# Attribute sums of a graph kernel, regrouped from two-strip pieces into three-strip units behind single tiles

## What is computed

```
h   = relu(layernorm(x));  H = batchnorm(h @ W.T + b)
deg = 1 + segment_sum(1, dst);  dinv = rsqrt(deg)
x   = x + relu(segment_sum(H[src] * dinv[src] * dinv[dst], dst) + H * dinv * dinv)
h   = relu(layernorm(x))
agg = segment_sum(edge_attr, dst)          # 206250 x 128 attributes, fp32
x   = x + (relu(relu([h, agg, u] @ W1 + b1) @ W2 + b2) @ W3 + b3)
```

## Time and profile before

| what | us |
|---|---|
| median of 3 runs | 1004.99 (1004.8 to 1006.06) |
| the profiled execution, its own time | 1005.95 |
| its span in the profile | 1004.2 |
| PE busy | 916.0 (91%), 9255 matmul instructions |
| POOL, DVE, ACT busy | 619.2, 578.5, 502.0 |
| strip sums of attributes, L1178, busy | 167.7 in 2240 instructions (attr_hot), 74.0 in 1000 (rows_hot) |
| strip sums of gathered rows, L1192, busy | 36.9 in 1000 instructions |

### The profile page before, as it was taken

The page is one execution under the profiler, slowest core; times in us unless marked ns, Lnnn a source line. Parts: engine busy times, 40 slices in busy tenths (PEclk is TensorE's granted clock), DMA queues, the critical chain, the costliest instruction groups (busy, mean ns, idle before and its releaser), DMA issues. The chain is left out here.

```text
span 1004.2 us, 23679 instructions
## 1 busy us (share of the span) xinstructions
PE 916.0 (91%) x9255; PEld 659.4 (66%) x9255; DVE 578.5 (58%) x1319; ACT 502.0 (50%) x867; POOL 619.2 (62%) x610
## 2 busy tenths in 40 slices
PE   2479559999999999999999999999999999997687
PEld 1357436777777777777777777777777777776455
DVE  6673756556555555556555655555565555542944
ACT  2135546455455555555555555555555555541485
POOL 5574562577777777777776177777777777710014
PEclk9567769999999999999999999999999999998989
DMA  7000464465565566565566355665655655623203
GB/s 183 14 1 1 130 211 157 135 205 169 187 204 173 182 203 194 164 201 178 178 201 189 127 171 186 204 194 165 201 177 178 202 182 174 204 64 92 53 21 108
DMA packets 87065, 154.65 MB, mean 154 GB/s; under 512 B 10967, under 2 KB 36885, under 8 KB 87005
## 3 DMA queue, kind: packets, MB, share of 16 engines
q1 hardware_dynamic: 71004, 121.11, 37.5%
q0 software_dynamic: 16000, 32.80, 10.9%
HBM read 147.46 MB, written 6.41 MB: 153 GB/s over the span
## 5 line engine op out<-in xcount | busy, mean ns | idle before, releaser
L957 POOL DMA_INDIRECT gathered<-scaled_h_table,index x500 | 534.6, 1069 | 232.4 <-issue 144.1
L969 ACT CAST counts_sb<-ps_counts 128x588 f16<-128x588 f32 x560 | 384.6, 688 | 367.7 <-PE ps_counts L1148 351.4
L1154 PE MATMUL ps_product<-counts_sb,table_sb 128*128 128x240 f16 x2744 | 436.0, 264 | 0.0
L1148 PE MATMUL ps_counts<-key_hot,lo_hot 128*128 128x294 bf16 x1120 | 329.2, 298 | 14.4 <-DVE key_hot L1031 12.3
L1154 PEld LDWEIGHTS ps_product<-counts_sb,table_sb 128*128 128x128 f16 x2744 | 266.0, 97 | 43.8 <-ACT counts_sb L969 0.2
L1031 DVE TENSOR_TENSOR key_hot<-key,iota_key 128x1176 bf16<-128x1176 f16 x280 | 213.4, 762 | 0.0
L1178 PE MATMUL ps_sums<-attr,attr_hot 128*32 128x128 f32 x2240 | 167.7, 280 | 2.9 <-DMA attr<-in_edge_attr_dram 2.9
L1089 DVE TENSOR_TENSOR acc<-acc,ps_product 128x96 f32 (+1 forms) x137 | 37.4, 273 | 223.2 <-PE ps_product L1208 187.2
L1148 PEld LDWEIGHTS ps_counts<-key_hot,lo_hot 128*128 128x128 bf16 x1120 | 111.4, 101 | 72.1 <-issue 24.1
L1026 DVE TENSOR_TENSOR lo_hot<-src_lo,iota_key 128x512 bf16<-128x512 f16 x280 | 118.6, 424 | 50.5 <-PE ps_counts L1148 50.4
L1178 PEld LDWEIGHTS ps_sums<-attr,attr_hot 128*32 128x32 f32 x2240 | 106.8, 110 | 48.6 <-issue 48.2
(11 more groups left out here) (219 smaller groups left out, 715.9 us busy)
## 6 DMA issues: line engine op xcount, KB each, us to landing
attr<-in_edge_attr_dram SPq DMA_DIRECT2D x80, 1280.0 KB
gathered<-scaled_h_table,index POOLq DMA_INDIRECT x500
acc<-in_x_dram SPq DMA_DIRECT2D x4, 768.0 KB, 9.0
scaled_h_table<-table_sb SPq DMA_DIRECT2D x12, 256.0 KB, 2.3
xs<-in_x_dram SPq DMA_DIRECT2D x12, 256.0 KB, 5.3
out_dram<-y_ring SPq DMA_DIRECT2D x12, 256.0 KB, 2.3
attr<-in_edge_attr_dram SPq DMA_DIRECT2D x2, 320.0 KB, 3.3
attr<-in_edge_attr_dram SPq DMA_DIRECT2D x1, 640.0 KB
```

The lines of the kernel that those rows point to most:

```text
L957: pool.indirect_dma_start(gathered[:, n % GATHERS, g, :], None, table, bass.IndirectOffsetOnAxis(ap=index[:, s * CG + g, t:t + 1], axis=0) ...
L969: act.copy(counts_sb[s % 2][:, :, 2 * k * WT:(2 * k + 2) * WT] .rearrange("p h (t n) -> p t h n", n=WT), ps_counts[n % 2][:, :, 0:KEYS].re ...
L1148: pe.matmul(ps_counts[pair % 2][:, c, 0:KEYS], lo_hot[:, b, part, :, c], key_hot[:, b, part, :, c], start=True, stop=True).then_inc(built, 1)
L1154: ins = pe.matmul(ps_product[side][:, 0:SLOTS], table_sb[:, h, low, :], counts_sb[side][:, h, :], start=(part == 0), stop=(part == 2 * NB ...
```

## The change

SUMS is now keyed by the tile q instead of the pair p, and its entries are (what, t, g), single matmuls. The 20 matmuls of a chunk are taken in the order of t and then g, three at a time (TRIPLES, seven of them, the last with two), and one such triple stands behind each of the tiles q = 2 to 8 (j = 0), 14 to 20 (j = 1) and 26 to 32 (j = 2). `sum_rows` stands behind q = 10, 12, 24, 35 and 37, where it stood behind q = 11, 13, 25, 35 and 37. Placements and `turn_product` keep their places. `sum_attr` takes one (t, g) and loses its loop. The number of matmuls is the same.

```diff
-        ALL, FIRST, SECOND = range(0, CG), range(0, CG // 2), range(CG // 2, CG)
-        SUMS = {1: [(0, FIRST, 0), (0, FIRST, 1)], 2: [(0, FIRST, 2), (0, FIRST, 3), (0, FIRST, 4)],
-                3: [(0, SECOND, 0), (0, SECOND, 1)], 4: [(0, SECOND, 2), (0, SECOND, 3), (0, SECOND, 4)],
-                5: [(3, ALL, 0)], 6: [(3, ALL, 1)],
-                7: [(1, FIRST, 0), (1, FIRST, 1)], 8: [(1, FIRST, 2), (1, FIRST, 3), (1, FIRST, 4)],
...
+        TRIPLES = [range(n, min(n + 3, CT)) for n in range(0, CT, 3)]
+        SUMS = {first + k: [(j, n // CG, n % CG) for n in triple]
+                for j, first in enumerate((2, 14, 26)) for k, triple in enumerate(TRIPLES)}
+        SUMS |= {q: [(3, t, 0)] for t, q in enumerate((10, 12, 24, 35, 37))}
...
-                            def sum_attr(s, k, a, held, loads, j, groups, t, first):
-                                if groups[0] == 0 and t == 0:
+                            def sum_attr(s, k, a, held, loads, j, t, g, first):
+                                if t == 0 and g == 0:
...
-                                for g in groups:
-                                    ins = pe.matmul(ps_sums[g * W:(g + 1) * W, 1, 0:P], hot[:, t, g, :],
-                                                    attr[:, held * CG + g, t * P:(t + 1) * P],
-                                                    start=(t == 0), stop=(t == GT - 1))
-                                if groups[-1] == CG - 1 and t == GT - 1:
+                                ins = pe.matmul(ps_sums[g * W:(g + 1) * W, 1, 0:P], hot[:, t, g, :],
+                                                attr[:, held * CG + g, t * P:(t + 1) * P],
+                                                start=(t == 0), stop=(t == GT - 1))
+                                if t == GT - 1 and g == CG - 1:
                                     ins.then_inc(summed, 1)
...
-                                    for what, groups, t in (SUMS if gathers(like) else FEWER_SUMS).get(p, ()):
...
+                                        for what, t, g in (SUMS if gathers(like) else FEWER_SUMS).get(q, ()):
```

More of the change, by code:

```diff
@@ L817, in gnn_kernel @@
         PART = [range(2 * NB * j // TILES, 2 * NB * (j + 1) // TILES) for j in range(TILES)]
-        ALL, FIRST, SECOND = range(0, CG), range(0, CG // 2), range(CG // 2, CG)
-        SUMS = {1: [(0, FIRST, 0), (0, FIRST, 1)], 2: [(0, FIRST, 2), (0, FIRST, 3), (0, FIRST, 4)],
-                3: [(0, SECOND, 0), (0, SECOND, 1)], 4: [(0, SECOND, 2), (0, SECOND, 3), (0, SECOND, 4)],
-                5: [(3, ALL, 0)], 6: [(3, ALL, 1)],
-                7: [(1, FIRST, 0), (1, FIRST, 1)], 8: [(1, FIRST, 2), (1, FIRST, 3), (1, FIRST, 4)],
[L826 to L831, removed]
+        TRIPLES = [range(n, min(n + 3, CT)) for n in range(0, CT, 3)]
+        SUMS = {first + k: [(j, n // CG, n % CG) for n in triple]
+                for j, first in enumerate((2, 14, 26)) for k, triple in enumerate(TRIPLES)}
+        SUMS |= {q: [(3, t, 0)] for t, q in enumerate((10, 12, 24, 35, 37))}
+        FEWER_SUMS = {q: [piece for piece in pieces if piece[0] < 2] for q, pieces in SUMS.items()}
         def gathers(s):
@@ L1249, in step @@
                                             multiply(side, PART[TILES - LAG + q])
-                                    for what, groups, t in (SUMS if gathers(like) else FEWER_SUMS).get(p, ()):
[L1251 to L1257, removed]
+                                        for what, t, g in (SUMS if gathers(like) else FEWER_SUMS).get(q, ()):
+                                            if what < 3:
+                                                a_like = ATTR_NO[like, what]
+                                                loads = i * 48 - (like + odd) * 24 + 16 * (a_like // 2 + 1)
+                                                sum_attr(s, k, a0 + what, a_like % 2, loads, what, t, g, first)
+                                            else:
+                                                sum_rows(k, t, gathered_before(like) == 0)
                                     if p == 3 and old:
```

## The result

| | before | after |
|---|---|---|
| median of 5 executions | 1004.99 | 1020.71 (1014.67 to 1021.02) |
| ratio to before, 95% interval | | 1.0142 (1.0121 to 1.0164) |
| profiled execution, own time | 1005.95 | 1014.67 |
| its span | 1004.2 | 1012.9 |
| first to last `turn_product`, below "the loop" | 735.1 | 744.5 |

The changed kernel is slower, as forecast: 15.7 us or 1.4% at the median, and the range held it, by 0.3 us. The profiled execution is the shortest of the five; the other four took 1020.62 to 1021.02. In four and six later executions on two other chips the same kernel took 1011.5 to 1017.6, with a ratio of 1.0089 both times (1.006 to 1.0118, and 1.0067 to 1.0111). So there the change costs about 0.9%, and the first group showed some 6 us more in four executions, of which there is no trace.

What follows compares the result with a forecast made beforehand. PE's own train of work was taken to bound the kernel. Attribute units +6.3, placements -4.2, the attr_hot wait +6.2 and the tie +0.3 gave +8.6 us, so 1013.6 us against a median of 1004.99, range 1005.5 to 1021.

Steps and rivals of the forecast that it cites:

- The bound: Main loop: a steady train of TensorE (PE) work sets its length, with PE busy 91% of the span.
- Part 1: Attribute sums: seven one-round units replace four pieces with ten rounds, +0.08 us per chunk, 79 chunks, +6.3 us.
- both rivals on the third strip: Attribute units: third strip slows the round by a quarter (about 1038 us, 0.05) or runs after the others (1114 us, 0.06).
- that of 2.38: Slower-round rival: the skill's 2.38 speedup for three column tiles makes a round 1.26 times as long; about 1038 us, 0.05.
- Part 2: Two placements a step now follow products instead of a piece, saving 0.09 and 0.08 us each: -4.2 us.
- Part 3: Second attribute chunk's first sum, behind q = 14: PE waits 0.25 us for attr_hot in 24 steps, +6.2 us.
- The tie at q = 24: One-hots for q = 24 come late by 0 to 0.05 us in 26 steps: +0.3 us in all.
- Sum: Whole kernel: +8.6 us on the profiled span of 1004.2, giving a median of 1013.6 us; a step 0.33 longer.
- The tell-tale signs: Profile after: units 0.45 to 0.46 over the tile, placements 0.43 and 0.21, PE waits for attr_hot 24 times.

Runs made afterwards that it cites:

- fours: Changed kernel with five units of four strip matmuls per chunk in place of seven of three: 966.87 us, ratio 0.9615 to the kernel before.
- rows_old: Changed kernel with the gathered rows (sum_rows) back at q = 11, 13, 25, 35 and 37: 1014.99 us, ratio 1.0123 to the kernel before.
- late15: Changed kernel with the second chunk's seven units behind q = 15 to 21, not 14 to 20: 1009.95 us, ratio 1.0048 to the kernel before.

## Why the prediction was right, and where it was not

- **The bound** was PE's own train of work, and it still is; ScalarE and GpSimd wait for it as before. Right.
- **Part 1, +6.3.** The unit was put at 0.45 to 0.46 and is 0.45, the three strips run side by side, and both rivals on the third strip fell, that of 2.38 with them; fours shows it for four strips as well. The Trainium skill's rule in "TensorE: Matmul & The Clock Gate", section The mechanism, that weight loads overlap running matmuls only across row groups, does not hold for these column strips: the unit's six loads take 0.15 us from 402.20 on, while its matmuls run from 402.21 for 0.42.
- **Part 2, -4.2.** 0.44 for the placement where 0.43 stood, 0.21 for the dense one where 0.21 stood, and rows_old gives back 0.07 a step where 0.09 stood. Right within the rounding of two decimals.
- **Part 3, +6.2.** The place, the count of 24 and the mechanism were right. The distances were 1.59 and 1.54 (411.33 and 411.28 after the build at 409.74) where 1.58 and 1.53 stood. The hand-over was a little too small: in this step attr_hot ends at 411.33 and the unit starts at 411.61, 0.28, and in the other looped steps it is 0.22 to 0.26, mostly 0.24, where 0.20 stood. So the 22 looped steps are held for about 0.29 each where 0.25 stood. The other two of the 24 are written out and not looped, and their hand-over is 0.05 to 0.06: step 15 is held for 0.44, as forecast, and step 27, which the prediction had counted as looped, for only 0.10. Together that is about 6.9 us. The waits view gives 5.2 us for 23 times, 0.23 each, as it counts from PE's modelled end; late15 gains 6.5 without the wait and the tie, net of the 1 us that it gives back.
- **The tie at q = 24, +0.3.** It was the term most undersized. q = 23 takes 418.74 - 418.36 = 0.38 in place of 0.33, in the looped steps, so about 1 us in all.
- **Sum.** +8.6 stood, +9.4 came in the loop (+9.3 against the profiles on other chips). A step grew from 28.15 to about 28.55, 0.40 where 0.33 stood: 0.24 for the units, -0.17 for the placements, 0.29 for the wait and 0.04 for the tie, by the means over the looped steps. 1013.6 lies by the 1013.12 and 1015.15 of the later groups and 7 below the first median of 1020.71. That gap is not in any term of the sum, and the experiments didn't reproduce it. That the range, which ended at 1021, still held this median is luck: its upper end was made of a longer wait and a costlier third strip, and neither came.
- The tell-tale signs came as written, with one wait fewer in PE's list than the 24 forecast, since that of step 27 is too short to stand there. PE's two waits for ScalarE (0.8 us) are no new sign; the kernel before has them too.

## What to carry to other kernels

Price a regrouping of column strips as visits plus rounds: here a visit costs 0.23 us and a round of fp32 matmuls 0.22 whether it fills two strips or four, so a regrouping that trades a round for a visit gains nothing, and one that fills all strips gains in both, as long as PE sets the time. When an operation is moved by one tile, follow its one-hot back to the event that both engines count from, and compare the two distances with the hand-over added; a few tenths of slack are easily spent. And once the first engine is faster, look who had just kept pace: with units of four a saving of 50 us in place of 67 came, since VectorE's row and the gathers set the time in places.

## What the runs showed of the hardware

- Four fp32 strip matmuls at once cost 0.01 us more than three (0.46 and 0.45 over the tile).
- In the looped steps, whose order shows a register instruction ahead of the waiting matmul, it takes 0.22 to 0.28 us from the end of VectorE's attr_hot to the first strip matmul (411.33 to 411.61 is the longest), against 0.05 to 0.06 in the two steps that are written out (15 and 27; the earlier trace rows has it for step 15 before). That the register instruction makes the difference is likely, but was not tried by itself.
- The kernel before took 1222.6 us on one chip and, at the median, 1004.2 to 1006.0 on the others. The changed kernel's trace on that chip has pauses of 0.3 to 0.8 us between matmuls that wait for nothing, and there the kernels with denser strips were the slowest. Units of four were faster than the kernel before on the three other chips that ran them, and slower on that one.
- The start of the program, the same code up to the first gather, takes 125.6 to 132.2 us in eleven profiles, while the loop of one kernel repeats to 0.3 us.
